# Layer 2's score pass: q kept in PSUM, gathered k in a ring of four halves, indices cast once, four product banks

## The reference, cut to what matters

```python
q = (x @ Wq_w + Wq_b)[dst]
k_base = (x @ Wk1)[src] + k_rel[edge_type] + Wk_b
score_base = jnp.sum(q * k_base, axis=-1)
scores = (score_base[:, None] + q @ v_rule.T) * scale
...
proj = jnp.einsum('nd,rdo->nro', x, W_r)
msg = proj[src, edge_type] * attn_mean[:, None]
```

## Time and profile before

| what | us |
|---|---|
| median of 3 runs (6835.92 to 6838.4) | 6837.18 |
| the profiled execution | 6846.75 |
| its span | 6845.0 |
| POOL busy in the span | 4793.0 |
| DVE busy in the span | 3805.6 |
| first gather of the score pass begins, last one ends | 3503.2, 4544.8 |

### The profile page before, as it was taken

How to read it: one execution, slowest core, us unless ns; L and a number is a source line. 1 busy time by engine, 2 the same in 40 slices (tenths; PEclk the granted TensorE clock), 3 DMA queues, 4 the chain that set the end, 5 groups by cost and what they waited for, 6 DMA issues and landing times. The chain is left out here.

```text
span 6845.0 us, 30054 instructions
## 1 busy us (share of the span) xinstructions
PE 1145.8 (17%) x5022; PEld 824.4 (12%) x5022; DVE 3805.6 (56%) x7908; ACT 1088.3 (16%) x2657; POOL 4793.0 (70%) x4901
## 2 busy tenths in 40 slices
PE   6446661000000000000267720000000001000000
PEld 5445651000000000000133310000000001000000
DVE  8999997344544434443456677776343453333336
ACT  1054441000000100000144410000000023222223
POOL 0077777777777677777767777777777777777774
PEclk9975555555555555555589965555555555555555
DMA  3091002244444334343369853324443432333332
GB/s 58 1 365 31 2 2 68 61 113 106 112 107 113 104 103 108 101 108 102 94 222 324 322 188 118 114 79 107 106 106 104 108 84 66 110 103 110 103 110 71
DMA packets 555015, 772.02 MB, mean 113 GB/s; under 512 B 120363, under 2 KB 431457, under 8 KB 535369
## 3 DMA queue, kind: packets, MB, share of 16 engines
q0 software_dynamic: 157328, 283.52, 18.5%
q1 hardware_dynamic: 379284, 375.57, 17.0%
q10 hardware_dynamic: 18210, 111.02, 4.2%
HBM read 357.57 MB, written 412.16 MB: 112 GB/s over the span
## 5 line engine op out<-in xcount | busy, mean ns | idle before, releaser
L2526 POOL DMA_INDIRECT l2s_krow<-table_k,l2s_idx x784 | 775.7, 989 | 266.2 <-issue 258.5
L957 POOL DMA_INDIRECT l2z_rows<-proj,l2z_idx x784 | 767.9, 979 | 250.5 <-issue 238.3
L957 POOL DMA_INDIRECT l0z_rows<-table,l0z_idx x784 | 744.1, 949 | 249.0 <-issue 238.6
L805 POOL DMA_INDIRECT l3z_rows<-table,l3z_idx x784 | 740.7, 945 | 249.3 <-issue 225.5
L957 POOL DMA_INDIRECT l1z_rows<-table,l1z_idx x784 | 740.8, 945 | 247.7 <-issue 238.6
L1948 POOL DMA_INDIRECT first_sj<-scores,first_atdst x488 | 510.6, 1046 | 160.2 <-issue 160.2
L2481 PE MATMUL l2s_bank<-l2o_wr,l2s_fed 128*128 128x512 f32 x800 | 382.3, 634 | 122.7 <-ACT l2s_fed L2505 106.1
L990 DVE TENSOR_TENSOR l1z_msg<-l1z_rows,l1z_factors 128x1024 f32<-128x1024 f32 (+1 forms) x50 | 60.0, 1200 | 555.0 <-DMA l1z_rows<-table,l1z_idx 555.0
L2463 DVE SCALAR_TENSOR_TENSOR l2s_qrow<-l2s_qrow,g_dokeep,l2s_zrow 128x82 f32<-128x82 f32 x1568 | 345.3, 296 | 6.4 <-DMA l2s_qrow<-table_q,l2s_first 5.8
L990 DVE TENSOR_TENSOR l2z_msg<-l2z_rows,l2z_factors 128x1024 f32<-128x1024 f32 (+1 forms) x50 | 60.0, 1200 | 515.0 <-DMA l2z_rows<-proj,l2z_idx 514.6
L2002 PE MATMUL sd_lfound<-first_terms,sd_lhot 128*128 128x100 f32 x1184 | 276.0, 428 | 266.8 <-ACT sd_lhot L2020 266.8
(11 more groups left out here) (591 smaller groups left out, 4878.0 us busy)
## 6 DMA issues: line engine op xcount, KB each, us to landing
proj<-l2s_proj ACTq DMA_DIRECT2D x100, 1024.0 KB, 6.0
spread_q<-prep_zero SPq DMA_DIRECT2D x98, 656.0 KB
l2s_zrow<-spread_q SPq DMA_DIRECT2D x98, 656.0 KB, 4.4
prefix<-l0z_acc SPq DMA_DIRECT2D x196, 256.0 KB, 3.3
prefix<-l1z_acc SPq DMA_DIRECT2D x196, 256.0 KB
prefix<-l2z_acc SPq DMA_DIRECT2D x196, 256.0 KB
prefix<-l3z_acc SPq DMA_DIRECT2D x48, 1040.0 KB, 4.1
l0z_rows<-table,l0z_idx POOLq DMA_INDIRECT x784, 2.6
```

The costliest lines, as they stand in the source:

```text
L805: nc.gpsimd.indirect_dma_start(out=rows[:, k % RING, u, :], out_offset=None, in_=table, in_offset=bass.IndirectOffsetOnAxis(ap=idx[:, lo + ...
L957: nc.gpsimd.indirect_dma_start(out=rows[:, k % RING, c * (hi - lo) + u, :], out_offset=None, in_=table, in_offset=bass.IndirectOffsetOnAxi ...
L2526: nc.gpsimd.indirect_dma_start(out=krow[:, h, u, :], out_offset=None, in_=g.table_k, in_offset=bass.IndirectOffsetOnAxis(ap=idx[:, h, u:u ...
```

## The change

q's 128 columns and the other 36 are accumulated apart: the 128 in a PSUM tile (`query`, two halves, four banks), the 36 in SBUF (`tail`). So each edge takes an instruction of 128 and one of 36 columns in place of two of 82, and the product reads k from SBUF and q from PSUM. All indices are cast in one instruction of 784 columns before the pass; the casts per half are gone. `krow` becomes a ring of four halves, and POOL waits for the product of four halves earlier. The load of `zrow` waits for the copy of the rule terms two halves earlier. The products of nodes and relation matrices pass through four PSUM banks, and PE waits for the copy out of each bank.

```diff
-                        hold(eng, zgot[h], i * 16 + 16)
-                        for u in range(U):
-                            for f in range(2):
...
-                                w = slice(f * QROW // 2, (f + 1) * QROW // 2)
-                                prev = qrow[:, h, u - 1, w] if u else qrow[:, 1 - h, U - 1, w]
-                                chain.add(v.scalar_tensor_tensor(qrow[:, h, u, w], prev, order.keep[:, bass.ds(i * 16 + 8 * h + u, 1)],
-                                                                 zrow[:, h, u, w], ALU.mult, ALU.add))
-                        hold(eng, got[h], i * (16 * U) + 16 * U)
-                        chain.add(v.tensor_tensor(prod[:], krow[:, h], qrow[:, h, :, 0:D], ALU.mult))
...
-                        v.tensor_copy(idx[:, h], g.src[:, bass.ds(i * 16 + 16 + 8 * h, U)]).then_inc(idx_ready[h], 1)
+        query = s.ps("query", [P, 2, U, D])
+        bank = [s.ps(f"bank{k}", [P, wide]) for k in range(ring)]
+                v.tensor_copy(idx[:], g.src[:, 0:NC]).then_inc(indexed, 1)
...
+                        chain.add(v.scalar_tensor_tensor(query[:, h, u], before, keep, zrow[:, h, u, 0:D], ALU.mult, ALU.add))
+                        if u:
+                            chain.until(1)
+                        chain.add(v.scalar_tensor_tensor(tail[:, h, u], after, keep, zrow[:, h, u, D:QROW], ALU.mult, ALU.add))
+                    chain.until()
+                    eng.wait_ge(got[m % ring], 16 * U * (m // ring + 1))
+                    v.tensor_tensor(prod[:], krow[:, m % ring], query[:, h], ALU.mult).then_inc(multiplied_k, 1)
...
+                    v.tensor_copy(qv[:, :, c].rearrange("p a j -> p j a"), tail[:, h, :, TYPES:rest]).then_inc(spread, 1)
...
+                        if b or k >= ring:
+                            pe.wait_ge(copied, b * parts + k - ring + 1)
...
+                    if m >= ring:
+                        hold(pool, multiplied_k, m - ring + 1)
...
+                    if m >= 2:
+                        sp.wait_ge(spread, m - 1)
```

More of the change, by code:

```diff
@@ L2420, in scores_and_projections @@
 def scores_and_projections(nc, name, g, order, base, qv, xT, wr):
-    banks, wide = 8, TYPES * D // 8
-    assert STEPS == NB - 1
+    parts, ring, wide = 8, 4, TYPES * D // 8
+    count, rest = NC // U, QROW - D
     with Space(nc, name) as s:
-        krow = s.sb("krow", [P, 2, U, D])
+        krow = s.sb("krow", [P, ring, U, D])
         zrow = s.sb("zrow", [P, 2, U, QROW])
-        qrow = s.sb("qrow", [P, 2, U, QROW])
+        tail = s.sb("tail", [P, 2, U, rest])
+        lead = s.sb("lead", [P, QROW])
         prod = s.sb("prod", [P, U, D])
@@ new lines, in _ @@
+                v.tensor_copy(first[:], g.dst[:, 0:1]).then_inc(indexed, 1)
+                v.tensor_copy(idx[:], g.src[:, 0:NC]).then_inc(indexed, 1)
+                eng.wait_ge(led, 16)
+                for m in range(count):
+                    h, c = m % 2, slice(m * U, (m + 1) * U)
+                    eng.wait_ge(zgot[h], 16 * (m // 2 + 1))
+                    for u in range(U):
+                        keep = order.keep[:, m * U + u:m * U + u + 1]
+                        if m + u == 0:
+                            before, after = lead[:, 0:D], lead[:, D:QROW]
+                        elif u == 0:
+                            before, after = query[:, 1 - h, U - 1], tail[:, 1 - h, U - 1]
+                        else:
+                            before, after = query[:, h, u - 1], tail[:, h, u - 1]
+                        if u:
+                            chain.until(1)
+                        chain.add(v.scalar_tensor_tensor(query[:, h, u], before, keep, zrow[:, h, u, 0:D], ALU.mult, ALU.add))
+                        if u:
+                            chain.until(1)
+                        chain.add(v.scalar_tensor_tensor(tail[:, h, u], after, keep, zrow[:, h, u, D:QROW], ALU.mult, ALU.add))
+                    chain.until()
+                    eng.wait_ge(got[m % ring], 16 * U * (m // ring + 1))
+                    v.tensor_tensor(prod[:], krow[:, m % ring], query[:, h], ALU.mult).then_inc(multiplied_k, 1)
+                    chain.add(v.tensor_tensor(pick[:], bc_mid(g.iota[:, 0:TYPES], U), bc_last(g.type[:, c], TYPES), ALU.is_equal))
+                    v.tensor_copy(qv[:, :, c].rearrange("p a j -> p j a"), tail[:, h, :, TYPES:rest]).then_inc(spread, 1)
+                    eng.wait_ge(multiplied_k, m + 1)
+                    chain.until()
+                    chain.add(v.tensor_reduce(part[:, 0], prod[:], AX, ALU.add))
+                    chain(v.tensor_tensor(pick[:], pick[:], tail[:, h, :, 0:TYPES], ALU.mult))
+                    chain(v.tensor_reduce(part[:, 1], pick[:], AX, ALU.add))
+                    chain.add(v.tensor_tensor(base[:, c], part[:, 0], part[:, 1], ALU.add))
@@ L2477, in _ @@
             @block.tensor
             def _(pe):
[L2479 to L2487, removed]
+                for b in range(NB):
+                    pe.wait_ge(feed, b + 1)
+                    for k in range(parts):
+                        if b or k >= ring:
+                            pe.wait_ge(copied, b * parts + k - ring + 1)
+                        nc.tensor.matmul(bank[k % ring][:], fed[:], wr[:, k * wide:(k + 1) * wide], start=True, stop=True).then_inc(multiplied, 1)
@@ L2506, in _ @@
                 for h in range(2):
                     act.wait_ge(stored[h], 16 * NB)
[L2508 to L2513, removed]
@@ L2514, in _ @@
-                for h in range(2):
-                    act.wait_ge(stored[h], 16 * (NB + 1))
             @block.gpsimd
             def _(pool):
[L2519 to L2527, removed]
+                pool.wait_ge(indexed, 2)
@@ new lines, in _ @@
+                nc.gpsimd.indirect_dma_start(out=lead[:], out_offset=None, in_=g.table_q,
+                                             in_offset=bass.IndirectOffsetOnAxis(ap=first[:, 0:1], axis=0)).then_inc(led, 16)
+                for m in range(count):
+                    if m >= ring:
+                        hold(pool, multiplied_k, m - ring + 1)
+                    for u in range(U):
+                        j = m * U + u
+                        nc.gpsimd.indirect_dma_start(out=krow[:, m % ring, u, :], out_offset=None, in_=g.table_k,
+                                                     in_offset=bass.IndirectOffsetOnAxis(ap=idx[:, j:j + 1], axis=0)).then_inc(got[m % ring], 16)
```

60 lines of the change are left out of this document (19 added, 41 removed).

## The result

The changed kernel takes 6783.34 us (median of 4 runs, 6782.47 to 6786.27), beside 6837.79 us for the kernel before on the same chip (4 runs). The ratio is 0.9927, with a 95% interval of 0.9915 to 0.9939.

A forecast was written before the change was run, and what follows sets the result against it. POOL, writing gather descriptors, was taken as the bound, the score pass 62 us over its floor. -17.2 - 7.0 - 5.7 + 5.3 + 0.2 = -24.4 us gave a median of 6813 us, range 6789 to 6827.

The forecast's parts named there:

- The six stalls: Score pass: POOL's idle times without a releaser, 112 gathers apart, 21.6 us beyond the usual, were forecast to stay.
- The product: Score pass, first stage: 25 gathers delayed by the product of k and q lose their excess, 17.2 us gained.
- something else delayed the gathers: Rival: the product was not the cause, or the delay only moves; only index waits go, 6832 us, chance 0.08.
- The accumulation: Score pass: gathers beside the accumulation of q lose 7.0 of 11.8 us in excess; bounds 0 and 11.8.
- The index waits: Score pass: POOL's 13 waits for indices go, because the ring lets it run ahead, 5.7 us gained.
- The marks: Score pass, first stage: the unchanged marking of types in SBUF meets more gathers, 6.3 us against 1.0, 5.3 lost.
- The lock-in rival: Every half of the score pass pays 0.24 us beside a mark, 18.2 us lost, 6826 us, chance 0.11.
- The stalls go too: Rival: the score pass's six stalls vanish as well, another 21.6 us gained, 6791 us, chance 0.18.
- first condition: In the stalls rival: the six stalls need VectorE reading two SBUF tiles, so they vanish with the change.
- second condition: In the stalls rival: the six stalls need the hand-over in two halves, so they vanish with the change.
- VectorE, the cast, the banks, SP's loads, POOL's wait: Score pass edits forecast to set no length: VectorE's half at most 8.6 us under POOL's 10.0; the cast loses 0.2 us.
- The sum's upper end: The 6822 us reached with the bounds of the accumulation and of second-stage marks, 4 us less or 8 more lost.

## Why the prediction was wrong

The direction and the mechanisms were right, the size was not, and the step that failed is "The six stalls I leave as they are". It was costed at nothing and was worth 21.6 us of the 30 that were missed. Point by point:

- **The product, 17.2 us gained: right.** No gather passes 1.21 us in the changed kernel, and q back in SBUF brings 19.1 us of them back. The rival that something else delayed the gathers fell with that one line of diff. The Trainium skill (SBUF — State Buffer, "Who interferes with whom") holds here in its rule on two SBUF inputs. Its inferred remark on a probe in which tensor_tensor did not stall DMA does not carry over to these gathers, which read their row numbers from SBUF: the gather of 1.84 us waited for a tensor_tensor, and a second such product brought some up to 1.98.
- **The accumulation, 7.0 taken: too small.** The gathers beside it lost 11.8 - 1.2 = 10.6 us of excess. The eight instructions of 36 columns that still read two SBUF tiles cost hardly anything; so neither the count of instructions (5.9) nor that of columns (9.2) was the measure. With the pair back in SBUF it is 7.1 us.
- **The index waits, 5.7 gained: right.** They are gone. With casts per half in a ring of four they cost 5.6 again.
- **The marks, 5.3 lost: too large.** 31 gathers meet one, with 6.8 us in excess, where 23 had 5.3: 1.5 lost, and in the second profiled execution of the same kernel only 20 do, with 4.4 us. In the first stage ten do (2.05 us), not the 30 of a gather that comes at random. I had taken the gathers' phase there as random. That the landings keep the two engines in step in this stage too would explain it, but that was not tested by itself. The lock-in rival (18.2 lost) did not come.
- **The stalls: wrong, and the rival "The stalls go too" came true** (6791, chance 0.18). Its first condition, VectorE reading two SBUF tiles, was not it, as the 3.51 us of an idle VectorE in the earlier trace rows had said rightly. But I let that one row speak against the second condition as well, though I had read from it that a stall's end follows a landing; all 18 stalls on two semaphores bear that out. The row that should have decided was in the earlier trace rows: l1z issues as many gathers and has no stall. It hands its landings over on six semaphores in turn and the score pass did so on two, and that difference I read as belonging to the tiles. "The same 784 gathers" was true of the data and not of how they signal. Two against four semaphores, with nothing else different, are 1004.8 against 985.8 us of the pass.
- **VectorE, the cast, the banks, SP's loads, POOL's wait: rightly costed at nothing.** The pair takes 352 + 245 = 597 ns where 0.59 us was the bound; in the timeline, though, the next pair begins before this one has ended, so a half is 7.17 us and not 8.6. DMA share in the first stage rose from 0.89 to 0.92 and POOL waited 0.6 us in all for the product.
- **The sum's upper end: added up wrongly.** With both bounds that stand beside it (7.0 us for the accumulation, 8 for the marks) it is 6828 and not 6822. The time came out at the other end, so nothing hangs on it.

In numbers: -24.4, less 21.6 for the stalls, 3.6 more from the accumulation and 3.8 less lost to the marks, is -53.4; the median moved by 54.5 and the pass by 55.2.

## What to carry to other kernels

When two passes issue the same instructions and only one of them stalls, compare everything around the instructions, the semaphores on which they signal included, before the stall is called a property of the instruction. Where POOL (GpSimd) issues gathers without pause, let VectorE read at most one operand from SBUF beside it, and count the landings on four semaphores in turn rather than on one or two: that costs no memory, and here it took 19.0 us from the pass where q in PSUM took 25.2. A stall that no row explains belongs in the range at its full price, on top of the other terms' bounds.

## What the runs showed of the hardware

An accumulation of 128 columns that reads and writes PSUM takes 352 ns, and the same one in SBUF 344 with q back there: the place of q cost VectorE 8 ns an instruction.
